# Layer 0 of a compressed interaction network on one NeuronCore: three of its seven product tiles computed in three fp32r passes over high and low halves

## The reference

```
e  = stack([tbl_f[ids[:, f]] for f in range(39)], axis=1)            # (512, 39, 16)
X0 = Xi = e
for W, b in ((W0, b0), (W1, b1), (W2, b2)):                          # W0: (128, 39*39), W1, W2: (128, 39*128)
    Wr = W.reshape(128, 39, Xi.shape[1])
    Xi = einsum('hjk,bjd,bkd->bhd', Wr, X0, Xi) + b[None, :, None]   # (512, 128, 16)
    res.append(Xi.sum(axis=2))
h = concatenate(res + [dense_ctx], axis=1)                           # (512, 400)
h = maximum(h @ W_top1 + b_top1, 0); h = maximum(h @ W_top2 + b_top2, 0); y = h @ W_top3
```

## Time and profile before

| what | value |
|---|---|
| median of 3 runs | 669.59 us (668.69 to 670.15) |
| the profiled execution | 670.7 us |
| its span, first to last instruction | 668.9 us |
| mean granted TensorE clock | 0.995 |
| PE busy | 644.9 us, 96% of the span |
| PEld busy | 479.0 us, 72% |
| DVE busy | 458.9 us, 69% |
| ACT busy | 480.0 us, 72% |
| POOL busy | 497.0 us, 74% |

### The profile page before, as it was taken

How to read it: one execution, slowest core, us unless ns; L and a number is a source line. 1 busy time by engine, 2 the same in 40 slices (tenths; PEclk the granted TensorE clock), 3 DMA queues, 4 the chain that set the end, 5 groups by cost and what they waited for, 6 DMA issues and landing times.

```text
span 668.9 us, 11234 instructions
## 1 busy us (share of the span) xinstructions
PE 644.9 (96%) x2676; PEld 479.0 (72%) x2676; DVE 458.9 (69%) x1183; ACT 480.0 (72%) x1737; POOL 497.0 (74%) x467
## 2 busy tenths in 40 slices
PE   3599999999999999999999999999999999999998
PEld 1387677777777777777787777777776777779773
DVE  1367777778686968777725786868687877774920
ACT  1457678878787879697815787878796978784912
POOL 5779888979797988888835797979888886553710
PEclk9989999999999999999999999999999999999999
DMA  6643515151514233251500514132241404002000
GB/s 159 140 100 80 124 26 118 36 120 13 128 27 102 54 75 79 44 111 34 119 11 2 119 13 108 25 81 51 46 85 28 103 10 118 4 4 93 2 0 1
DMA packets 68264, 43.32 MB, mean 65 GB/s; under 512 B 49483, under 2 KB 61710, under 8 KB 66458
## 3 DMA queue, kind: packets, MB, share of 16 engines
q1 hardware_dynamic: 56870, 38.04, 25.4%
q0 software_dynamic: 5184, 1.29, 2.3%
q10 hardware_dynamic: 6158, 3.45, 2.0%
HBM read 39.58 MB, written 1.96 MB: 62 GB/s over the span
## 4 chain that ended last, share of the span: by engine, by line
PE 94%; issue 2%; DVE 1%; DMA 1%; ACT 1%; ACTq 0%; POOLq 0%; POOL 0%; DVEq 0%
PE a_ps L704 40%; PE d_ps L704 25%; PE quad_ps L655 14%; PE quad_ps L758 5%; PE g_ps L745 5%; PE g_ps L814 1%; DMA g_sb<-w_dram 1%; PE quad_ps L672 1%; PE a_ps L871 1%; PE quad_ps L659 1%; PE d_ps L842 1%; ACT parts L930 0%; DVE parts L551 0%; DVE x2t L563 0%; PE a_ps L842 0%
## 5 line engine op out<-in xcount | busy, mean ns | idle before, releaser
L930 ACT ACTIVATE parts<-a_ps,xt 128x128 f32<-128x128 f32 x1536 | 424.1, 383 | 129.7 <-PE a_ps L704 115.3
L551 DVE SCALAR_TENSOR_TENSOR parts<-d_ps,xt,parts 128x128 f32<-128x128 f32 x704 | 201.7, 343 | 108.9 <-PE d_ps L704 98.9
L311 POOL TENSOR_TENSOR parts<-parts 128x512 f32<-128x512 f32 x128 | 163.5, 1293 | 99.3 <-ACT parts L930 98.0
L704 PE MATMUL a_ps<-w_hi,x_hi 128*128 128x512 f32 x384 | 181.3, 472 | 1.5 <-issue 1.5
L311 POOL TENSOR_TENSOR left<-parts 128x512 f32<-128x512 f32 x128 | 167.3, 1323 | 7.5 <-ACT parts L930 5.9
L285 POOL DMA_INDIRECT emb<-tables_dram,rows_now x150 | 144.0, 960 | 25.3 <-issue 18.5
L704 PE MATMUL a_ps<-w_hi,x_lo 128*128 128x512 f32 x384 | 152.4, 397 | 0.6 <-issue 0.6
L704 PE MATMUL a_ps<-w_lo,x_hi 128*128 128x512 f32 x384 | 151.4, 394 | 0.0
L704 PE MATMUL d_ps<-w_hi,x_hi 128*128 128x512 f32 (+1 forms) x256 | 127.0, 496 | 0.9 <-DVE parts L551 0.9
L655 PE MATMUL quad_ps<-products,w_sb 117*128 117x512 f32 (+1 forms) x210 | 107.4, 592 | 0.0
L704 PE MATMUL d_ps<-w_lo,x_hi 128*128 128x512 f32 (+1 forms) x256 | 97.8, 382 | 0.6 <-ACT xt L908 0.6
(11 more groups left out here) (72 smaller groups left out, 428.4 us busy)
## 6 DMA issues: line engine op xcount, KB each, us to landing
shifted<-x_rows SPq DMA_DIRECT2D x45, 312.0 KB
shifted<-x_rows SPq DMA_DIRECT2D x45, 234.0 KB
diag<-xt SPq DMA_DIRECT2D x240, 4.9 KB
rows<-x_rows SPq DMA_DIRECT2D x45, 78.0 KB
emb<-tables_dram,rows_now POOLq DMA_INDIRECT x150
w_sb<-w_dram SPq DMA_DIRECT2D x6, 384.0 KB
shifted<-x_first SPq DMA_DIRECT2D x12, 136.5 KB
g_sb<-w_dram ACTq DMA_DIRECT2D x2, 768.0 KB
```

The lines of the kernel that those rows point to most:

```text
L311: nc.gpsimd.tensor_tensor(to, parts[:, i % 2, now:now + GF, :], parts[:, i % 2, more:more + GF, :], ALU.add).then_inc(pool_added, 1)
L551: nc.vector.scalar_tensor_tensor(now, d_ps[d % D_RING][:, H * at:H * (at + 1)], xt[:, u, i, j:j + 1], before, ALU.mult, ALU.add).then_inc( ...
L704: return nc.tensor.matmul(bank[:, 0:H * len(fields)], x[:, u, 128 * i:128 * (i + 1)], w[:, fields[0]:fields[-1] + 1, :].rearrange("p j h - ...
L930: last = nc.scalar.activation(parts[:, i % 2, 2 + GF * a + at, :], a_ps[(NA * i + a) % A_RING][:, H * at:H * (at + 1)], ACT.Copy, scale=xt ...
```

## The change

In chunks 3 to 15 (`SPLIT_FROM`), three of layer 0's seven tiles (1, 3 and 5) are multiplied in three fp32r passes. For each such tile ScalarE copies the products into `products_hi` (`high_products`), VectorE subtracts that from the products into `products_lo` (`low_products`), and TensorE runs w0_hi with products_hi, w0_lo with products_hi and w0_hi with products_lo into the same bank. The weights' halves are made once, in chunk 1, by one ScalarE copy and one VectorE subtraction of 117 x 384. The tables change too: the seven tiles' places on TensorE, the places of `high_x1` (ScalarE, (3, 0) to (3, 2)) and `low_x1` (VectorE, (3, 1) to (3, 2)) in the chunks that have no tables of their own, and in the last chunk the place of VectorE's two small subtractions for the context columns (`LOW_CTX_AT`, from (2, 3) to (3, 0)).

```diff
-L0_AT = {(1, 5): 0, (1, 7): 1, (2, 1): 2, (2, 3): 3, (2, 5): 4, (2, 8): 5, (3, 0): 6}
+L0_AT = {(1, 5): 0, (2, 0): 1, (2, 1): 2, (2, 6): 3, (2, 7): 4, (3, 1): 5, (3, 2): 6}
...
-CLEAR_CTX_AT, HIGH_CTX_AT, LOW_CTX_AT = (0, 2), (2, 2), (2, 3)
-HIGH_X1_AT, LOW_X1_AT, SUM_X1_AT, BIAS_Z1_AT = (3, 0), (3, 1), (0, 0), (1, 2)
+CLEAR_CTX_AT, HIGH_CTX_AT, LOW_CTX_AT = (0, 2), (2, 2), (3, 0)
+HIGH_X1_AT, LOW_X1_AT, SUM_X1_AT, BIAS_Z1_AT = (3, 2), (3, 2), (0, 0), (1, 2)
...
+SPLIT, SPLIT_FROM = (1, 3, 5), 3
+NS = len(SPLIT)
+HIGH_AT, LOW_AT = {(1, 1): 1, (2, 0): 3, (2, 2): 5}, {(1, 1): 1, (2, 0): 3, (2, 2): 5}
+HIGH_W0_AT, LOW_W0_AT = (0, 1), (0, 1)
...
+            def low_products(m, t):
+                k = SPLIT.index(t)
+                dve.wait_ge(products_hi_ready, NS * (m - SPLIT_FROM) + k + 1)
+                nc.vector.tensor_tensor(products_lo[0:PK, k, :], products[0:PK, t, :], products_hi[0:PK, k, :].bitcast(F32),
+                                        ALU.subtract).then_inc(products_lo_ready, 1)
...
+                            if n + 1 >= SPLIT_FROM and (i, d) in LOW_AT:
+                                low_products(n + 1, LOW_AT[i, d])
+                        if n == 1 and (i, d) == LOW_W0_AT:
+                            dve.wait_ge(w0_hi_ready, 1)
+                            nc.vector.tensor_tensor(w0_lo[:, :, :], w0_sb[:, SPLIT[0]:SPLIT[-1] + 1:2, :],
+                                                    w0_hi[:, :, :].bitcast(F32), ALU.subtract).then_inc(w0_lo_ready, 1)
...
             def layer0(m, t):
+                rows = PK if t < QT - 1 else QT_LAST
+                if t in SPLIT and not (isinstance(m, int) and m < SPLIT_FROM):
+                    k = SPLIT.index(t)
+                    pe.wait_ge(products_lo_ready, NS * (m - SPLIT_FROM) + k + 1)
+                    for w, x in ((w0_hi, products_hi), (w0_lo, products_hi), (w0_hi, products_lo)):
+                        mm = nc.tensor.matmul(quad_ps[:, :], w[:, k, :], x[0:PK, k, :], start=False, stop=False)
+                    mm.then_inc(products_used, 1)
+                    return
                 pe.wait_ge(products_ready, QT * (m - 1) + t + 1)
-                rows = PK if t < QT - 1 else QT_LAST
                 nc.tensor.matmul(quad_ps[:, :], w0_sb[0:rows, t, :], products[0:rows, t, :],
...
+            def high_products(m, t):
+                k = SPLIT.index(t)
+
+                act.wait_ge(products_ready, QT * (m - 1) + t + 1)
+                nc.scalar.copy(products_hi[0:PK, k, :], products[0:PK, t, :]).then_inc(products_hi_ready, 1)
...
+                        if not last and n + 1 >= SPLIT_FROM and (i, a) in HIGH_AT:
+                            high_products(n + 1, HIGH_AT[i, a])
+                        if n == 1 and (i, a) == HIGH_W0_AT:
+                            nc.scalar.copy(w0_hi[:, :, :], w0_sb[:, SPLIT[0]:SPLIT[-1] + 1:2, :]).then_inc(w0_hi_ready, 1)
```

More of the change, by code:

```diff
@@ L71 @@
 BUFS = 2
-L0_AT = {(1, 5): 0, (1, 7): 1, (2, 1): 2, (2, 3): 3, (2, 5): 4, (2, 8): 5, (3, 0): 6}
-PART_L0_AT = {(1, 8): 0, (2, 0): 1, (2, 2): 2, (2, 5): 3, (2, 8): 4, (3, 0): 5, (3, 2): 6}
+L0_AT = {(1, 5): 0, (2, 0): 1, (2, 1): 2, (2, 6): 3, (2, 7): 4, (3, 1): 5, (3, 2): 6}
+PART_L0_AT = {(1, 8): 0, (2, 0): 1, (2, 2): 2, (2, 6): 3, (2, 8): 4, (3, 1): 5, (3, 2): 6}
 LATE_L0_AT = {(1, 7): 0, (2, 0): 1, (2, 1): 2, (2, 3): 3, (2, 5): 4, (3, 0): 5, (3, 2): 6}
@@ L185, in build @@
         products = sb("products", [128, QT, CW])
+        products_hi, products_lo = sb("products_hi", [128, NS, CW], F32R), sb("products_lo", [128, NS, CW], F32R)
+        w0_hi, w0_lo = sb("w0_hi", [PK, NS, H], F32R), sb("w0_lo", [PK, NS, H], F32R)
         x1_hi = sb("x1_hi", [128, 2, CW], F32R)
@@ L233, in build @@
         products_ready, products_used = sem("products_ready"), sem("products_used")
+        products_hi_ready, products_lo_ready = sem("products_hi_ready"), sem("products_lo_ready")
+        w0_hi_ready, w0_lo_ready = sem("w0_hi_ready"), sem("w0_lo_ready")
         x1_hi_ready, x1_lo_ready = sem("x1_hi_ready"), sem("x1_lo_ready")
```

## The result

The changed kernel is slower: 672.15 us median (668.29 to 674.73, 11 runs) against 669.59 (668.39 to 670.61, 11 runs), ratio 1.0041, 95% interval 1.0027 to 1.0054. The forecast was 665.3, with a range of 662.0 to 668.9. The runs of the changed kernel spread over 6.4 us, those of the kernel before over 2.2: that spread is the first clue.

A forecast was written before the change was run, and what follows sets the result against it. TensorE was taken to bound the kernel. Tiles -6.4, late x1_lo +3.1 and the last chunk -1.0 summed to -4.3 us, so 665.3 us against the median 669.6, range 662.0 to 668.9.

The forecast's parts named there:

- Bound and pass price: TensorE sets the time; three passes cost 0.695 instead of 0.86 us a tile, over 39 tiles -6.4 us.
- ScalarE's copy: Copies of 117x512 to fp32r, three a chunk, about 0.652 us each, hidden in ScalarE's idle time.
- VectorE's undisturbed subtraction: Subtraction of 117x512 for a tile's low half, taken as 0.6 us when nothing disturbs it.
- Late x1_lo: At the next chunk's start TensorE's third matmul waits for x1_lo: 0.26 us in each of twelve chunks, +3.1 us.
- The rival that it costs nothing: Late x1_lo adds nothing at the chunk starts, leaving 662.2 us; chance 0.10.
- Last chunk: Context subtractions placed behind d-group 1 remove TensorE's 0.88 us idle time there: -1.0 us, bounds 0 and -1.3.
- Weights' halves: Made once in chunk 1 on ScalarE and VectorE: cost 0, at most +0.5 us.
- the disturbed subtraction: VectorE's subtractions for tiles 1, 3 and 5 beside GpSimd, 0.6 to 1.7 us each, cost TensorE 0.
- that 0.7: Slack in us before TensorE wants tile 3's low half in block 2; if gone, each chunk pays the excess.
- the tight one: Tile 3's subtraction in block 2, forecast to run from 438.8 to 439.4 and be wanted at 440.1.
- VectorE and GpSimd hold each other up: Rival at block 2, tile 3: TensorE waits 0.6 us a chunk over 13 chunks, giving 673.1 us; chance 0.12.

The follow-up runs named there:

- the PSUM operand: Changed kernel with VectorE's low-half subtraction reading rows_ps in PSUM instead of products_hi: 666.34 us, ratio 0.9958; with low_x1 back at (3, 1) as well: 664.07 us.
- the two runs with tables: Kernel before with the changed kernel's tables but no fp32r passes: 673.89 us; the same with each chunk's first g_block moved to block 2: 672.08 us.
- the two with PSUM operands: Changed kernel with the subtraction reading rows_ps in PSUM: 666.34 us; the same with each chunk's first g_block moved to block 2: 665.39 us.
- PSUM operand and moved `g_block`: Changed kernel with the subtraction reading rows_ps in PSUM and each chunk's first g_block moved to block 2: 665.39 us, ratio 0.9934.
- lowx: Changed kernel with low_x1 alone put back from (3, 2) to (3, 1): 673.15 us, ratio 1.0056 to the kernel before.

## Why the prediction was wrong

**Bound and pass price: right.** TensorE sets the pace in every version; three passes of 117 rows are 0.70, a tile saves 0.167, 39 tiles 6.5. (The matmul at 438.16, which the prediction calls tile 5's, is tile 3's by the table: it stands behind group 3 of block 2. The price is the same.)

**ScalarE's copy: right.** 643 ns on average against 0.652, hidden. VectorE's undisturbed subtraction is 0.68 rather than 0.6, which changes nothing.

**Late x1_lo: right.** 0.16 and 0.10 in each of the twelve chunks, 2.9 net in the traces against 3.1. The rival that it costs nothing is ruled out: undone beside the PSUM operand it gave 2.3 us in the times, and block 0 of each such chunk is 7.53 again instead of 7.77.

**Last chunk: right by the trace**, 1.14 in block 3 against 1.0; not measurable in the times.

**Weights' halves: right**, chunk 1 is 36.81 against 36.79.

**The step that failed** is the one on the disturbed subtraction: "I cost all this at **0**; its cover is that 0.7". Three things in it were wrong. It let tile 1's subtraction wait for the first of two adds and then run; in eight of 13 it lost to the second too, 2.15 in place of 1.1. It called tile 3 the tight one; tile 3 never made TensorE wait in these traces. And it dismissed tile 5: "falls where GpSimd starts DMAs or waits and has more than 1 us". VectorE, late after a double loss, reaches tile 5's subtraction some 0.4 us into a DMA start with a pair of adds behind it, takes 3.68, and has 1.1 us of slack where this needs 3.0. The price is 1.9 for each and, by the estimate above of three in an execution, 5.5 us or so, more than the whole forecast gain. The Trainium skill ("SBUF — State Buffer", section "SBUF: two separate sides") has the mutual lock for a whole instruction, and the pair with PSUM operands (679 ns each time) agrees; that the waiting side may lose twice in a row is what the runs add.

**The step that was missing.** I kept `g_block` where it was and priced nothing there, though I had taken 0.86 out of the block ahead of it. Its copies are released by ScalarE and issued by SyncE, neither of which became faster: in chunk 3 ScalarE's copy into `xt` ends 10.2 us into the chunk (before, 10.0), while TensorE reaches group 9 of block 1 at 15.6 instead of 16.2. So it now waits in three to six of chunks 3 to 10: 1.5 to 2.4 us in all in the five traces of the changed kernel, and 0.55 to 2.9 in the other versions that leave `g_block` in its place; 1.7 between the medians of the two runs with tables, 1.0 between the two with PSUM operands.

**The sum without both** was right: PSUM operand and moved `g_block` give 0.9934, 4.2 us below the kernel before, where the forecast had -4.3; its blocks, without the start-up, give -4.1. The rival "VectorE and GpSimd hold each other up" had the mechanism and, by luck, nearly the time, 673.1: it put it at the wrong tile, as a steady 0.6 a chunk rather than 1.9 now and then; 0.12 for it was too little, with two subtractions of 1.50 and 1.70 in the earlier trace rows the only ones beside GpSimd's adds in the trace to judge by.

**Open:** why the moment decides as it does. For tile 5 the boundary lies between 0.377 and 0.378 us behind the beginning of the DMA start, without an exception in 38. For tile 1 (same seven traces), counted from the first add's beginning, the 27 that began at 0.93 to 0.98 lost to both adds, the 21 that began at 1.003 or later got in between them, and of the 27 between 0.985 and 1.002 17 did. But arrival alone doesn't settle it: chunk 8's began at 0.69 to 0.70 and got in all seven times (1.15 long), lowx's at 0.76 to 0.82 lost all nine times. No run here varied that moment by itself or changed GpSimd's program, and none says why VectorE's and GpSimd's phases differ by these hundredths from one execution to the next.

## What to carry to other kernels

An operation whose duration depends on another engine is priced by its worst case at each of its places (here the whole run of adds, with the DMA start ahead of them), and the slack is asked for there, down the chain: the loss of one such operation shifts the next into another collision. When the engine that sets the pace loses work, look at every wait behind the cut, DMA copies too, since what they wait for didn't get faster. A spread that grows with a change can be a mechanism and not noise: here several traces of the same kernel, held against their times, named it.

## What the runs showed of the hardware

VectorE's subtraction of 117x512 with both operands in SBUF takes 0.68 alone. Beside GpSimd's adds of 1.3 it took 0.87 when it got in between two of them (the second add then took 1.75), 1.6 behind the rest of one, 2.1 to 2.4 behind two, and 3.5 to 3.7 when it began 0.378 us or more into a DMA start with two adds behind it; up to 0.377 it took 0.68. With one operand in PSUM it took 0.676 to 0.681 in 39 of 39 beside the same adds. It works the other way too: 29 DMA starts of GpSimd that began during such a subtraction for tile 5 took 1.32 to 1.42 us, and 20 that began during one with a PSUM operand took 0.97 to 0.98.
